# Three transformer blocks and a rotation on one core: the durations that order the engines' work are replaced

## What is computed

```
mod = silu(c) @ w_adaln + b_adaln                    # six rows per batch: shift, scale, gate, twice
h = modulate(ln(x), sh_msa, sc_msa); q, k, v = split(h @ w_qkv + b_qkv)     # 16 heads of 18
x = x + g_msa * (softmax(q k^T * hd**-0.5) v @ w_proj + b_proj)
xn = modulate(ln(x), sh_mlp, sc_mlp)
layer 0:   top 2 of 4 experts by xn @ w_gate;  moe = sum of cw * (gelu(xn @ w1[e] + b1[e]) @ w2[e] + b2[e])
layer 1:   attention over the 16 heads within one token (the heads are the sequence), one MLP
layer 2:   attention over the 256 tokens, as layer 0, one MLP
last:      U, _ = qr(P); R = expm(skew(silu(cond) @ W.T + b)); z = x U; x + (z R - z) U^T
```

## Time and profile before

| | us |
|---|---|
| median of 3 runs | 1294.09 (1289.55 to 1294.12) |
| the profiled execution | 1286.9, of which the span of instructions 1285.1 |
| TensorE busy | 1178.6 |
| VectorE, ScalarE, GpSimd busy | 903.0, 740.3, 451.8 |

### The profile page before, as it was taken

The page is one execution under the profiler, slowest core; times in us unless marked ns, Lnnn a source line. Parts: engine busy times, 40 slices in busy tenths (PEclk is TensorE's granted clock), DMA queues, the critical chain, the costliest instruction groups (busy, mean ns, idle before and its releaser), DMA issues.

```text
span 1285.1 us, 31567 instructions
## 1 busy us (share of the span) xinstructions
PE 1178.6 (92%) x12305; PEld 849.7 (66%) x12305; DVE 903.0 (70%) x2048; ACT 740.3 (58%) x1477; POOL 451.8 (35%) x818
## 2 busy tenths in 40 slices
PE   5778878879999999899999996999999999999998
PEld 3344445538887888677777784776766677576775
DVE  6999988864444333686766568777848979877454
ACT  5675867654454343376564565654657657676643
POOL 4322433642234122733212346242633432342220
PEclk9798979979999999899999997999999999999999
DMA  7697535475678867674455553322112101000002
GB/s 204 177 362 260 184 69 142 154 243 173 236 249 295 252 216 237 228 156 148 109 134 134 159 154 95 47 39 69 28 16 55 20 5 19 10 16 6 11 1 76
DMA packets 105161, 166.73 MB, mean 130 GB/s; under 512 B 42813, under 2 KB 89014, under 8 KB 98358
## 3 DMA queue, kind: packets, MB, share of 16 engines
q1 hardware_dynamic: 101670, 154.46, 42.0%
q0 software_dynamic: 3072, 9.97, 2.3%
q10 hardware_dynamic: 272, 0.29, 0.1%
HBM read 124.88 MB, written 35.34 MB: 125 GB/s over the span
## 4 chain that ended last, share of the span: by engine, by line
PE 73%; DVE 12%; issue 4%; ACT 4%; DMA 3%; POOL 2%; SPq 1%; DVEq 0%; ACTq 0%; POOLq 0%
PE P L1920 17%; PE P L1748 12%; PE P L1930 6%; PE P L1932 6%; PE P L1931 6%; PE P L1877 4%; DVE NM L2188 3%; PE P L1765 2%; PE P L1868 2%; PE P L1775 2%; PE P L1853 2%; PE P L1844 2%; POOL STG L2762 1%; ACT ARENA L2627 1%; PE P L1831 1%
## 5 line engine op out<-in xcount | busy, mean ns | idle before, releaser
L1920 PE MATMUL P<-XT,W 128*128 128x256 f16 x2394 | 278.5, 274 | 6.0 <-ACT W L2519 1.8
L1920 PEld LDWEIGHTS P<-XT,W 128*128 128x128 f16 x2394 | 230.2, 98 | 45.3 <-issue 10.2
L1930 PE MATMUL P<-W,H 128*128 128x288 f16 x684 | 196.1, 287 | 0.0
L1932 PE MATMUL P<-W,H 128*128 128x288 f16 x684 | 195.6, 286 | 0.0
L1931 PE MATMUL P<-W,H 128*128 128x288 f16 x684 | 195.6, 286 | 0.0
L2660 ACT ACTIVATE G<-P 128x512 f32<-128x512 f32 (+1 forms) x190 | 105.3, 554 | 152.2 <-PE P L1920 132.0
L2188 DVE TENSOR_REDUCE NM<-P 128x2 f16<-128x512 f32 x256 | 159.7, 686 | 16.5 <-PE P L1853 15.9
L2627 ACT ACTIVATE ARENA<-P 128x512 f32<-128x512 f32 x256 | 133.6, 609 | 50.7 <-PE P L1868 48.6
L1748 PE MATMUL P<-WQ,XT 128*128 128x288 f16 x1008 | 141.8, 291 | 6.8 <-issue 3.6
L2362 DVE TENSOR_TENSOR H<-G,H 128x512 f16<-128x512 f32 (+1 forms) x123 | 80.8, 668 | 80.1 <-ACT H L2661 79.7
L1748 PEld LDWEIGHTS P<-WQ,XT 128*128 128x128 f16 x1008 | 95.7, 99 | 41.2 <-issue 12.5
(11 more groups left out here) (384 smaller groups left out, 2266.0 us busy)
## 6 DMA issues: line engine op xcount, KB each, us to landing
W<-scr_w SPq DMA_DIRECT2D x22, 1440.0 KB, 6.5
W<-scr_w SPq DMA_DIRECT2D x22, 1368.0 KB, 6.2
XT<-scr_x SPq DMA_DIRECT2D x22, 320.0 KB, 7.4
scr_w<-W SPq DMA_DIRECT2D x4, 1440.0 KB, 8.6
scr_w<-W SPq DMA_DIRECT2D x4, 1368.0 KB, 9.0
scr_y<-TM SPq DMA_DIRECT2D x35, 144.0 KB, 4.0
scr_x<-XT SPq DMA_DIRECT2D x1, 4160.0 KB, 13.8
H<-in_L_w SPq DMA_DIRECT2D x9, 432.0 KB, 6.8
```

The costliest lines, as they stand in the source:

```text
L1920: ins = e.matmul(bank(st)[:, 256 * k:256 * k + 256], W1[:, w, m * 128:(m + 1) * 128], XT[:, b, x, :], start=i == 0, stop=i == 6)
L1930: e.matmul(o, hi, W2[:, 2 * m, :], start=False, stop=False)
L1932: ins = e.matmul(o, lo, W2[:, 2 * m, :], start=False, stop=m == 8)
```

## The change

Three edits. `SWITCH` goes from 3 to 4. A table `MEASURED` gives a duration per engine and kind for 83 kinds of step, and `SHARE` a factor of 1.18 for `gelu`. The last line of `do` before the step is appended puts this duration in place of the call's own one; the lane's clock has by then been advanced with the call's own duration, so that the first pass, the choice of engines and all rings but the PSUM banks stay as they were, and `by_readiness` and `from_the_end` see the new numbers. A kind that the table lacks keeps its number (`top_mm`, `s_mm`, `up_mm`, `h_lo`, `w_hi`, `w_lo` among them). One number stands for all steps of a kind: the three pieces of `down_mm` all get 1.191.

```
-SWITCH, STAY = 3, 0
+SWITCH, STAY = 4, 0
...
+MEASURED = dict(
+    pe=dict(av=1.035, t_av=0.958, t_bc=0.489, cond_mm=1.4, down_mm=1.191, qkv_mm=0.963, proj_mm=0.93, t_proj=2.0, tqk_T=0.54, top_T=0.21, r_mm=0.577),
...
+SHARE = dict(gelu=1.18)
...
             st.cost, st.deps = cost, [x for v in rest if isinstance(v, (Step, list, tuple)) for x in flat(v) if isinstance(x, Step)]
+            st.cost = MEASURED[lane.name].get(kind, cost * SHARE.get(kind, 1.0))
             lane.steps.append(st)
```

More of the change, by code:

```diff
@@ L42 @@
 SLACK, BIAS = -0.5, 0.2
+MEASURED = dict(
+    pe=dict(av=1.035, t_av=0.958, t_bc=0.489, cond_mm=1.4, down_mm=1.191, qkv_mm=0.963, proj_mm=0.93, t_proj=2.0, tqk_T=0.54, top_T=0.21, r_mm=0.577),
+    dve=dict(top=0.686, t_top=0.679, hh_step=1.458, m_lo=1.479, x_lo=1.356, full=1.594, mixed=1.489, m_hi=0.896, proj_gate=0.454, q_lo=0.452, k_lo=0.45,
+             t_norm=0.593, kt=0.679, qt=0.68, ln_aggr=0.178, av_norm=0.456, tq=1.213, tk=1.212, eo=0.453, ot=0.688, rows_lo=1.22, rows_hi=0.829, e_sq=0.681,
+             gx=0.96, xg=0.96),
+    act=dict(exps=0.61, t_exp=0.599, ln_z=1.259, hh_norm=0.605, full=1.672, q_hi=0.654, k_hi=0.652, x_hi=0.953, m_hi=1.025, v=0.418, tv=0.427, qt=1.021, kt=1.023,
+             tq=1.03, tk=1.034, ot=0.615, t_out=0.394, eo=0.41, rows_hi=0.696, gx=1.44, xg=1.44),
+    pool=dict(hh_root=1.472, x_add=0.835, ln_eps=0.619, ln_pow=0.753, ln_mean=0.337, got=2.04, sent=1.0, m_lo=2.538, rows_mod=3.11),
+    sp=dict(w_back=1.0, hh_row=0.557, w2_in=1.56, top_row=1.366, t_row=1.4, tv_in=1.735, y_out=0.442, gi_in=0.605, g1_in=0.468, g2_in=0.4, gm_in=0.394, rows_in=0.4,
+            tv_out=0.443, cond_out=0.583, w_keep=0.566, x_init=0.73, wp1_in=3.5))
+SHARE = dict(gelu=1.18)
 class Hold:
```

## The result

The changed kernel takes 1314.66 us (1311.52 to 1315.36), the kernel before 1292.81 beside it (1289.55 to 1294.12): a ratio of 1.018, 95% interval 1.0152 to 1.0205. It is slower by 22 us, where 1291 was predicted with a range of 1277 to 1303. The two profiled executions differ by 28.1 us in span; that of before (1286.9 us) lies 6 us under its median, so differences between the two traces read some 6 us larger than the difference of the medians.

The account below looks back on a forecast made before the run. TensorE was busy 1178.6 of 1285.1 us, so gains had to come from the other 106.5; VectorE bounds layer 0's attention. Terms -3 - 2 + 1 + 2 - 1 = -3 us on 1294.1 gave 1291 us, range 1277 to 1303.

Parts of the forecast that it names:

- everything else: In 291 to 512, 546 to 768 and 802 to 1248: better TensorE durations remove a few waits, -1 us, bounds -6 and +6.
- What the new durations are: Planner's table: means of one instruction, a correction for TensorE, not for overlapping VectorE and ScalarE; some gain, not a large one.
- rival (c): Whole kernel: another order but no better, since overlap is counted into the durations; 1294 to 1297 us, chance 0.15.
- Layer 0's attention: 32 to 291 us: 11 more VectorE instructions cost +5, 8 of 27.2 us of waits saved; -3 us, bounds -9 and +10.
- the marks of 292 and 296: End of layer 0's attention (first L1934): at 284 to 292 us the prediction is right, after 296 wrong.
- The first change of piece: 512 to 546 us: the exponential product's wait goes, TensorE waits 4.5 against 6.0; -2 us, bounds -6 and +3.
- The second change: 768 to 802 us: less cover from exponential products, more from up_mm and transposes, one more h_lo; +1 us, bounds -6 and +4.
- the 10 to 13 that were to show it right: Second change of piece, 768 to 802 us before: 10 to 13 us of waits were to confirm the prediction.
- The table switches: ScalarE: 12 more exp/gelu table loads of 1.28 us, mostly covered; +2 us, bounds 0 and 15.4.
- rival (b): Layers 1 and 2: table switches land on the path, 10 of 12 loads uncovered; +8 us, 1302 us, chance 0.20.
- rival (d): ScalarE: a table change holds it as much again beyond its load, all uncovered; 15 us more, 1306 us, chance 0.03.
- the 900 full microseconds: Stretches where TensorE is full: idle appearing there, or TensorE's busy time moving over 5 us, would prove the argument wrong.

Follow-up runs that it names:

- e16: Kernel before with its own durations, ScalarE's times 1.10 and VectorE's times 1.0625, SWITCH 3: 1310.9 us, ratio 1.018.
- e10: Kernel before with ScalarE's new durations alone, SWITCH 3: 1311.7 us, ratio 1.017.
- e12: Changed kernel with ScalarE's new durations times 0.86 and VectorE's times 0.91, so their sums match busy time: 1292.1 us, ratio 1.003.
- e13: Kernel before with TensorE's new durations alone, SWITCH 3: 1291.4 us, ratio 1.002.
- e1: Changed kernel with SyncE's own durations put back, in a disturbed group of runs: 1305.8 us, ratio 0.997.
- e3: Changed kernel with the down product's (down_mm) own duration put back, in a disturbed group of runs: 1310.8 us, ratio 1.001.
- e11: Kernel before with SyncE's new durations alone, SWITCH 3: 1303.6 us, ratio 1.012.
- e8: Kernel before with SWITCH 0 in place of 3, own durations kept (41 table loads for 33): 1296.3 us, ratio 1.005.
- e9: Changed kernel with STAY 10 in place of 0, new durations kept (31 table loads for 45): 1321.3 us, ratio 1.025.
- e14: Kernel before with each duration times a random number between 0.98 and 1.02, a second draw: 1293.7 us, ratio 1.006.
- e15: Kernel before with each duration times a random number between 0.98 and 1.02, a third draw: 1290.0 us, ratio 1.000.
- e17: The numbers of e12, each duration times a random number between 0.98 and 1.02: 1278.6 us, ratio 0.993.
- e5: Kernel before, unchanged, profiled once more in a disturbed group of runs: 1314.3 us, ratio 1.000.
- e6: Changed kernel, unchanged, profiled once more beside the kernel before on the same chip, in a disturbed group: 1330.9 us, ratio 1.011.
- e7: Changed kernel with each duration times a random number between 0.98 and 1.02, in a disturbed group: 1329.6 us, ratio 1.011.
- e18: The numbers of e12, with down_mm at its own cost by the count of its matmuls: 1290.5 us, ratio 1.001.

## Why the prediction was wrong, step by step

Two steps failed. The one that the traces show is the last term of the sum, "everything else": -1 with a bound of +6, where 21 to 24 us were lost. The one behind it, as far as the runs show, is the price of the overlap. I go through the steps in the prediction's order.

**What the new durations are: the fact was right, its price was wrong.** The prediction read from the earlier trace rows that 0.686 stood for 0.62 of occupancy and 0.61 for 0.52, called the planner "nearer the chip on TensorE, and no nearer on the two engines that evict", and expected "some gain from it and not a large one". It took the overstatement as a gain that is missing. It can be a loss: alone it costs 1.8% in one order (e16; e10 with ScalarE's alone 1.7%), without it the change is at 1.003 (e12), and the correction on TensorE that was to bring the gain brings nothing (e13, 1.002). That it was the whole cause of the loss is not shown (e1, e3 and e11 above). In rival (c) the same overlap was priced at 0 to +3 us, in the right direction and too small by seven times.

**Layer 0's attention (-3): about right in sum, by another way.** The first L1934 begins at 292.8 (before 291.6), between the marks of 292 and 296. VectorE's waits for other engines up to there add up to 27.3 us, not to 15 to 22; before had 27.2. The largest of them:

```profile
DVE NM L2202 <- PE P L1867: 4.1, 8, 1.1
DVE TM L2224 <- PE P L1762: 3.7, 5, 1.3
DVE QB L2130 <- ACT QB L2609: 3.2, 5, 1.2
DVE ARENA L2324 <- ACT ARENA L2573: 3.0, 1, 3.0
DVE ST L2117 <- POOL X L2824: 3.0, 1, 3.0
```

The 8.5 behind the maxima's matmul have halved, and of the 5.3 behind `cond_mm` 1.3 are left; but the waits for ScalarE and GpSimd, the last three of these rows and two smaller ones, add up to 11.9 us, where before had 3.7, and have taken their place. The 5 us more of VectorE work did not show (227.7 against 227.3 us busy). TensorE did 2220 matmuls by 292, before 2202 by 291; at equal work this is the 4.4 us that it is ahead at 288.

**The first change of piece (-2): right in TensorE's wait, wrong in its times.** Timeline of the changed kernel's GpSimd:

```profile
521.02 1.61 POOL L2776 DMA_INDIRECT STG<-scr_y,POSI  x1 [1.22 <-DMA TM<-scr_ada]
...
536.95 1.54 POOL L2824 TENSOR_TENSOR X<-X,STG 128x288 f32<-128x288 f32 x2
```

and of its TensorE:

```profile
536.28 1.20 PE L1955 MATMUL P<-EY 64*64 64x64 f32 x32
539.69 0.40 PE L1941 MATMUL P<-W,ONES 128*128 128x288 f16 x1 [2.22 <-issue]
```

The exponential product no longer waits for VectorE, as said; TensorE waits 2.22 and, ahead of the first projection, 1.99 us: 4.2 where 4.5 were worked out. But the twelve gathers start 8.7 us later than before (521.02 against 512.29), since a Householder step and a DMA stood ahead of them, and the adds with them (536.95 against 524.83). TensorE had other work in that time.

**The second change (+1): direction right, too small.** 784 to 830 holds 13.2 us of idle time and 768 to 784 another 3.2, 16.4 in all. Before has 12.6 in 756 to 802, its wait for W1 at 761.77 included. At equal work 6.5 us are lost from 704 to 864. The waits:

```profile
774.69 0.28 PE L1941 MATMUL P<-W,ONES 128*128 128x288 f16 x1 [1.59 <-DMA W<-scr_w]
788.61 13.30 PE L1934 MATMUL P<-XT,W 128*128 128x256 f16 x105 [6.25 <-ACT W L2533]
804.34 0.44 PE L1789 MATMUL P<-IDF,ARENA 128*128 128x128 f32 x2 [2.42 <-ACT ARENA L2573]
811.64 0.69 PE L1789 MATMUL P<-IDF,ARENA 128*128 128x128 f32 x2 [4.07 <-ACT ARENA L2573]
```

They add up to 14.3, above the 10 to 13 that were to show it right. `ln_z` costs 6.5 in two waits, where before it cost 6.9 in one. What grew is the last split of W1 (L2533): 6.25 us where the earlier trace rows had 1.83. The working looked at the exponential products and the `up_mm` that moved, and left this wait out as unchanged.

**The table switches (+2): right, and rival (b) false.** 45 loads are there, and the largest wait of TensorE for exponentials of layer 1 behind one is 1.96 us. The load and the exponentials behind it:

```profile
598.65 1.28 ACT L2601 ACT_TABLE_LOAD   x1
599.94 1.08 ACT L2601 ACTIVATE ARENA<-P 128x512 f32<-128x512 f32 x2
```

No gap, as in the earlier trace rows; the instruction ahead of the load ends at 598.63. So rival (d) is false too. (The Trainium skill's drain of 1.38 us per switch, in "ScalarE: Activation LUTs", What ACT_TABLE_LOAD costs, shows in neither trace; and e8 and e9 show that the count of switches doesn't set the time.)

**Everything else (-1, bounds -6 and +6): the term that was missed in size.** This is the step of the sum that failed. In 546 to 722 TensorE is idle for 17.5 us where before was for 1.7 with about the same work. At equal work, busy time included, the change loses 21.2 us from 544 to 704 and 3.3 from 864 to the end: +21 to +24 where the bound was +6. The prediction said itself that idle time in the 900 full microseconds would refute it, or a busy time of TensorE that moves by more than 5 us (it moved by 12.5). The bound was drawn from what is missing there today, "15.4 us ... in waits of mostly under 2 us". That limits a gain. It doesn't limit a loss: a stretch in which nothing waits has everything to lose when all of its steps are laid down anew.

**The chances.** 0.23 stood on slower by over 0.5%, nearly all of it for a mechanism that the runs refute. A second order of the same quality would have scattered by 0 to +0.6% (e8, e14, e15), since the list of before was already a favourable one; that was not in the sum either.

## What to carry to other kernels

When durations from a trace go into a planner, take an engine's busy time divided by its count, not the mean length of an instruction, and hold the planned sum of each engine against its busy time: the orders with ScalarE planned 16% and VectorE 10% above their busy time ran 1.8 to 2.5% slower here (the change, e9, e16; e1 and e3 in a disturbed group are the exceptions), and with both within 6% all orders of the undisturbed groups but e11 came within 0.6% of before or under it. The planned end says nothing on it: the old numbers plan an end at 1237 us and run in 1285, the new ones plan 1317 and run in 1313, and make the worse kernel. Where a search lays all steps down anew, redraw it a few times by scattering the durations by 2% before any change of numbers is judged: the draws lie 0.6% (old numbers) to 1% (e12 and e17) apart, and the best of them (e17, 0.993) is the only order of the undisturbed groups that ran clearly faster than before.

## What the runs showed of the hardware

**Engines stand still while GpSimd's indirect DMAs run, in some groups of runs and not in others.** In e5 the kernel before loses 28.0 us against its first trace by 576 us of work, and 0.2 after. VectorE's largest wait in 240 to 275 of e5:

```profile
DVE NM L2188 <- remote: 11.9, 1, 11.9
```

and all that the DMA queues moved in 256 to 267 (packets, MB, share):

```profile
q0 software_dynamic: 400, 1.31, 32.6%
```

"remote" is a wait for which the profile finds no releaser in this kernel. The only DMA traffic in those 11 us is that of the software queue, GpSimd's scatters of layer 0's tokens. In e6 it is ScalarE, at the gathers of the first change of piece, which GpSimd issues from 533.11 on:

```profile
533.11 1.50 POOL L2776 DMA_INDIRECT STG<-scr_y,POSI  x1 [1.33 <-DMA TM<-scr_ada]
...
547.40 0.95 POOL L2776 DMA_INDIRECT STG<-scr_y,POSI  x1 [0.30 <-issue]
...
550.62 0.60 ACT L2674 ACTIVATE G<-P 128x512 f32<-128x512 f32 x1 [17.79 <-remote]
```

ScalarE's own last instruction ended at 532.8, and nothing came from it until the last of the gathers had been issued. In the traces of e1 to e7 such waits add up to between 31 and 56 us over all engines; in the first traces of both kernels and in e8 to e18 there are none. One chip appears in both kinds of group, so it isn't the chip. What the engines wait for is not shown.

**Long gaps can cost twice.** Between before and the change 12.5 of 28.1 us are busy time of the same matmuls, at a mean granted clock of 0.964 and 0.958; e17 gains by busy time alone (1168.9 against 1178.6) at equal idle time, with a clock of 0.979. Two `up_mm` rows of 14 matmuls in the changed kernel:

```profile
805.05 2.52 PE L1934 MATMUL P<-XT,W 128*128 128x256 f16 x14
...
826.89 1.70 PE L1934 MATMUL P<-XT,W 128*128 128x256 f16 x14
```

The first stands behind waits of 6.25 and 2.42 us in the second change, and the granted clock in 806 to 815 is 0.50 of full; in 820 to 830 it is 1.00. Shorter waits show it little: 546 to 722 has 17.5 us of idle time, one wait of 4.0 us and the others of about 2 us and less, at a clock of 0.98.
